# A 16-head attention of a decoder rewritten from a loop over sequences to one unrolled stream of 64 head pairs

## The reference, cut to what matters

```python
h = layernorm(x)                                  # no weights, eps 1e-5
q = (h @ Wq + bq) / 8;  k = ctx @ Wk + bk;  v = ctx @ Wv + bv     # 128 -> 1024 features, 16 heads of 64
p = softmax(q @ k.T + mask)                       # per sequence and head, 256 x 256
x = x + concat_heads(p @ v) @ Wo + bo             # 1024 -> 128
```

## Time and profile before

| | us |
|---|---|
| median of 3 runs (2844.6 to 2848.43) | 2846.11 |
| the profiled execution | 2847.98 |
| its span in the profile | 2846.2 |
| PE busy in the span | 1904.2 (67%) |
| PEld busy | 1116.7 (39%) |
| DVE busy | 1594.2 (56%) |
| ACT busy | 951.7 (33%) |
| POOL busy | 152.7 (5%) |

### The profile page before, as it was taken

The page is one execution under the profiler, slowest core; times in us unless marked ns, Lnnn a source line. Parts: engine busy times, 40 slices in busy tenths (PEclk is TensorE's granted clock), DMA queues, the critical chain, the costliest instruction groups (busy, mean ns, idle before and its releaser), DMA issues. The chain is left out here.

```text
span 2846.2 us, 37625 instructions
## 1 busy us (share of the span) xinstructions
PE 1904.2 (67%) x12470; PEld 1116.7 (39%) x12470; DVE 1594.2 (56%) x5577; ACT 951.7 (33%) x1872; POOL 152.7 (5%) x162
## 2 busy tenths in 40 slices
PE   3897689367864489923234777767798888558922
PEld 1554334234543345511123444444454444333410
DVE  5665368444444466667666666565623333457854
ACT  1553267231211145422002444444432222116721
POOL 2110021000000032000000000000000000002100
PEclk9998799678976689955557998898998989559965
DMA  3100120000000011000001000000000000002000
GB/s 89 22 13 1 45 35 12 8 1 0 0 6 0 26 23 24 2 11 0 38 0 79 4 4 4 4 7 4 5 1 0 0 0 6 0 14 28 13 0 15
DMA packets 22000, 38.52 MB, mean 14 GB/s; under 512 B 2176, under 2 KB 17536, under 8 KB 20864
## 3 DMA queue, kind: packets, MB, share of 16 engines
q1 hardware_dynamic: 20160, 35.47, 5.2%
q10 hardware_dynamic: 1728, 1.57, 0.4%
HBM read 23.40 MB, written 1.05 MB: 9 GB/s over the span
## 5 line engine op out<-in xcount | busy, mean ns | idle before, releaser
L434 DVE TENSOR_REDUCE L_xattn_nmax<-ps 128x4 f32<-128x1024 f32 x192 | 234.6, 1222 | 126.3 <-PE ps L663 124.8
L543 ACT ACTIVATE L_xattn_probs<-ps 128x1024 f32<-128x1024 f32 x192 | 196.6, 1024 | 126.7 <-PE ps L696 125.2
L2122 ACT ACTIVATE wide_pr<-wide_sc,wide_nm 128x256 f32<-128x256 f32 x256 | 127.9, 500 | 133.0 <-DVE wide_nm L2074 113.5
L1179 DVE SCALAR_TENSOR_TENSOR moe_z_sb<-ps,weights,moe_a_sb 128x512 f32<-128x512 f32 x64 | 47.7, 750 | 173.8 <-ACT moe_a_sb L1197 173.7
L2070 DVE CUSTOM_DVE_ANT_0 wide_sc<-ps,wide_mask 128x256 f32<-128x256 f32 x256 | 97.3, 417 | 67.3 <-PE ps L2162 67.3
L1231 PE MATMUL ps<-moe_z_sb,weights 128*128 128x512 f32 x256 | 123.5, 628 | 8.9 <-DVE moe_z_sb L1179 8.9
L2173 PE MATMUL ps<-const,wide_pr 128*128 128x128 f32 x512 | 90.1, 302 | 36.9 <-DVE wide_pr L2080 36.9
L810 PE MATMUL ps<-L_xattn_parts,lay 128*128 128x512 bf16 x288 | 96.9, 406 | 18.3 <-ACT L_xattn_parts L620 17.2
L712 PE MATMUL ps<-L_xattn_probs,values 128*32 128x256 f32 x1536 | 102.8, 385 | 1.6 <-ACT L_xattn_probs L543 1.6
L2162 PE MATMUL ps<-wide_k,wide_q 64*128 64x256 f32 x512 | 71.9, 405 | 45.4 <-DVE wide_nm L2074 37.9
L309 POOL TENSOR_TENSOR L_xattn_rest<-L_xattn_full,L_xattn_parts 128x512 f32<-128x512 f32 x24 | 27.7, 1156 | 1312.9 <-ACT L_xattn_parts L620 1312.9
(11 more groups left out here) (485 smaller groups left out, 4322.6 us busy)
## 6 DMA issues: line engine op xcount, KB each, us to landing
keys<-L_xattn_parts SPq DMA_DIRECT2D x126, 64.0 KB
weights<-in_packed_L_ffn SPq DMA_DIRECT2D x2, 2608.0 KB, 12.2
keys<-L_attn_parts SPq DMA_DIRECT2D x42, 64.0 KB
weights<-in_packed_L_xattn SPq DMA_DIRECT2D x2, 1316.0 KB, 7.1
wide_mask<-in_mask SPq DMA_DIRECT2D x8, 256.0 KB, 2.7
const<-in_packed_const SPq DMA_DIRECT2D x1, 1677.5 KB, 9.7
weights<-in_packed_L_ffn SPq DMA_DIRECT2D x1, 1540.5 KB, 10.4
weights<-in_packed_L_ffn SPq DMA_DIRECT2D x1, 1540.0 KB, 6.6
```

The lines of the kernel that those rows point to most:

```text
L434: v.tensor_reduce(nm, ps[:, BANK_M:BANK_M + 2, :].rearrange("p j (t n) -> p j t n", t=2), AX.X, ALU.max, negate=True).then_inc(S("m_used"), 1)
L543: a.activation(probs[:, s % RING, :, :, :].rearrange("p j t n -> p j (t n)"), ps[:, BANK_P:BANK_P + 2, :], ACT.Exp, scale=HD ** -0.5)\
L2122: ins = a.activation(pr[:, h % 2, qt, :], sc[:, h % 2, qt, :], ACT.Exp, bias=nm[:, h % 2, qt:qt + 1], accum_out=sums[:, h % 2, qt:qt + 1])
```

## The change

The loop and its blocks go. The sublayer is one block, unrolled over 64 slots (8 sequences of 8 head pairs), and every engine walks through the places tau = -16 to 79. In place s PE turns the probabilities of slot s-2 (8 transposes), makes the scores of slot s+1 in one pair of banks, and weighs slot s-2; DVE masks slot s (4 operations), copies the first head of the turned slot s-2, negates the maxima of slot s (one operation for the pair), and normalises slot s-1 (4 operations); ACT copies the weighed slot s-3, the second head of the turned slot s-2, and takes the exponentials of slot s (4 operations). So half of the copies of turned probabilities move from DVE to ACT.

Beside this, in the same places: q and k of slot s+2 are projected into one bank (one pair of matmuls per place) and copied by ACT in the next place; V of the next sequence is projected in positions 1 to 4 through one bank, and copied by DVE in positions 2 to 5; that bank also takes the transposed LayerNorm output of the next sequence (position 5) and the product with Wo of the sequence before (positions 6 and 7), which DVE adds to x at position 0 of the window after. The statistics of the LayerNorm of sequence n+2 are interleaved with DVE's operations in positions 4 and 5, the normalised rows are made by ACT in position 6 instead of by DVE, and the bias bo is added to x by POOL. The context is read in place rather than copied. The scaling of bq and the load of the next weights move into the same block, and the masks have two buffers and are loaded ahead, behind the next weights in SP's queue. The lines that the change adds, with "..." where some are left out (declarations of buffers, Newton's iteration, which is as before, and the removed lines, which are printed above):

```diff
+    SLOTS = SEQS * M
+    BANK_S, BANK_T, BANK_V, BANK_A, BANK_B = 0, 2, 4, 6, 7
+    QK = 6
+    half = [slice(DK * j, DK * j + DK) for j in range(2)]
...
+        places = [Place(tau, M, SEQS) for tau in range(-2 * M, SLOTS + 2 * M)]
+        def projected(tau):
+            n, t = divmod(tau, M)
+            m = n + (t >= QK)
+            return (m if 0 <= m < SEQS else None), (t - QK) % M
+        with C.turn() as block:
...
+                at = ks.index(k)
+                if at + 1 < len(ks):
+                    load_weights(C, sp, ks[at + 1], packed)
+                for m in range(SEQS):
+                    if m >= 2:
+                        sp.wait_ge(S("scores_used"), 4 * M * (m - 1))
+                    sp.dma_start(mask[:, m % 2, :, :], maskd[:, m * 2 * SEQ:(m + 1) * 2 * SEQ]
+                                 .rearrange("p (t n) -> p t n", t=2)).then_inc(S(("even_mask", "odd_mask")[m % 2]), 16)
...
+                g.wait_ge(C.weights_loaded[k], 32)
+                g.tensor_scalar(bq[:, :], w("bq"), DK ** -0.5, None, ALU.mult).then_inc(S("bias_scaled"), 1)
+                for m in range(SEQS):
+                    g.wait_ge(S("xn_ready"), 2 * (m + 1))
+                    x3 = xp(m).rearrange("p (t d) -> p t d", d=D)
+                    g.tensor_tensor(x3, x3, bcast(w("bo"), 1, [P, 2, D]), ALU.add).then_inc(S("bo_added"), 1)
...
+                def prepare(m):
+                    for t in range(2):
+                        yield L.tick(v.bn_stats(stats[:, t, :], C.x[:, m * SEQ + t * D:m * SEQ + (t + 1) * D]))
+                    L.settle()
+                    one = mv[:, m % 2, :, :]
+                    for t in range(2):
+                        yield L.tick(v.bn_aggr(one[:, t, :], stats[:, t, :]))
+                    L.settle()
+                    first, shift = rstd[:, m % 2, 0, :], rstd[:, m % 2, 1, :]
+                    yield from newton(first, one[:, :, 1], 2)
+                    yield v.scalar_tensor_tensor(shift, one[:, :, 0], -1.0, first, ALU.mult, ALU.mult)\
+                        .then_inc(S("rstd_ready"), 1)
+                def masked(s, j):
                     for qt in range(2):
+                        v.tensor_tensor_reduce(out=sc[:, s % 2, j, qt, :], in0=ps[:, BANK_S + j, qt * SEQ:(qt + 1) * SEQ],
+                                               in1=mask[:, s // M % 2, qt, :], scale=1.0, scalar=-3.0e38, op0=ALU.add,
+                                               op1=ALU.max, accum_out=mx[:, s % 2, 2 * j + qt:2 * j + qt + 1])\
+                         .then_inc(S("scores_used"), 1)
+                v.wait_ge(C.weights_loaded[k], 32)
+                side = iter(())
+                for p in places:
+                    s = p.tau
+                    m = p.job(4, 2)
+                    if m is not None:
+                        side = prepare(m)
+                    live = 0 <= s < SLOTS
+                    if live:
+                        v.wait_ge(S("scores_ready"), s + 1)
+                        if s % M == 0:
+                            v.wait_ge(S(("even_mask", "odd_mask")[s // M % 2]), 16 * (s // M // 2 + 1))
+                        masked(s, 0)
+                        next(side, None)
+                        masked(s, 1)
+                    next(side, None)
+                    if 0 <= s - 2 < SLOTS:
+                        v.wait_ge(S("prT_ps"), s - 1)
+                        v.tensor_copy(prT[:, s % 2, 0, :, :].rearrange("p t n -> p (t n)"), ps[:, BANK_T, :])\
+                         .then_inc(S("prT_first"), 1)
+                    next(side, None)
+                    if live:
+                        v.wait_ge(S("scores_used"), 4 * (s + 1))
+                        v.tensor_scalar(nm[:, s % 2, :], mx[:, s % 2, :], -1.0, None, ALU.mult).then_inc(S("masked"), 1)
+                    if 0 <= s - 1 < SLOTS:
+                        r = s - 1
+                        v.wait_ge(S("exp_done"), r + 1)
+                        inverted = L.tick(v.reciprocal(inv[:, r % 2, :], sums[:, r % 2, :]))
+                        next(side, None)
+                        L.upto(inverted)
+                        for j in range(2):
+                            for qt in range(2):
+                                one = pr[:, r % 3, j, qt, :]
+                                v.tensor_scalar(one, one, inv[:, r % 2, 2 * j + qt:2 * j + qt + 1], None, ALU.mult)\
+                                 .then_inc(S("normalised"), 1)
+                                next(side, None)
+                    for n in range(4):
+                        m = p.job(n + 2, 1)
+                        if m is not None:
+                            v.wait_ge(S("v_proj"), 4 * m + n + 1)
+                            if m >= 2 and n == 0:
+                                v.wait_ge(S("pv_ready"), M * (m - 1))
+                            cols = slice((n % 2) * 512, (n % 2) * 512 + 512)
+                            v.tensor_tensor(V[:, m % 2, n // 2, cols], ps[:, BANK_B, :], w("bv")[:, cols], ALU.add)\
+                             .then_inc(S("v_ready"), 1)
+                    m = p.job(0, -2)
+                    if m is not None:
+                        v.wait_ge(S("out_ready"), m + 1)
+                        v.wait_ge(S("bo_added"), m + 1)
+                        v.tensor_tensor(xp(m), xp(m), ps[:, BANK_B, 0:SEQ], ALU.add).then_inc(S("added"), 1)
+                    if p.t == 5:
+                        for _ in side:
+                            pass
...
+                a.wait_ge(C.weights_loaded[k], 32)
+                a.wait_ge(S("bias_scaled"), 1)
+                for p in places:
+                    s = p.tau
+                    if 0 <= s - 3 < SLOTS:
+                        r = s - 3
+                        a.wait_ge(S("pv_ready"), r + 1)
+                        if r >= 2 * M and r % M == 0:
+                            a.wait_ge(S("out_ready"), r // M - 1)
+                        a.activation(attT[:, r // M % 2, r % M, :], ps[:, BANK_V + r % 2, 0:SEQ], ACT.Copy)\
+                         .then_inc(S("attT_ready"), 1)
+                    m = p.job(6, 1)
+                    if m is not None:
+                        a.wait_ge(S("hT_ps"), m + 1)
+                        a.activation(hT[:, :], ps[:, BANK_B, 0:SEQ], ACT.Copy).then_inc(S("hT_ready"), 1)
+                    m, u = projected(p.tau - 1)
+                    if m is not None:
+                        a.wait_ge(S("qk_proj"), M * m + u + 1)
+                        a.activation(q[:, u % 4, :], ps[:, BANK_A, 0:SEQ], ACT.Identity, bias=bq[:, u:u + 1],
+                                     scale=DK ** -0.5)
+                        a.activation(kk[:, u % 4, :], ps[:, BANK_A, SEQ:2 * SEQ], ACT.Identity,
+                                     bias=w("bk")[:, u:u + 1]).then_inc(S("qk_copied"), 1)
+                    if 0 <= s - 2 < SLOTS:
+                        a.wait_ge(S("prT_ps"), s - 1)
+                        a.activation(prT[:, s % 2, 1, :, :].rearrange("p t n -> p (t n)"), ps[:, BANK_T + 1, :], ACT.Copy)\
+                         .then_inc(S("prT_second"), 1)
+                    if 0 <= s < SLOTS:
+                        a.wait_ge(S("masked"), s + 1)
+                        for j in range(2):
+                            for qt in range(2):
+                                n = 2 * j + qt
+                                ins = a.activation(pr[:, s % 3, j, qt, :], sc[:, s % 2, j, qt, :], ACT.Exp,
+                                                   bias=nm[:, s % 2, n:n + 1], accum_out=sums[:, s % 2, n:n + 1])
+                        ins.then_inc(S("exp_done"), 1)
+                    m = p.job(6, 2)
+                    if m is not None:
+                        a.wait_ge(S("rstd_ready"), m + 1)
+                        if m:
+                            a.wait_ge(S("hT_ps"), m)
+                        for t in range(2):
+                            a.activation(xn[:, t, :], C.x[:, m * SEQ + t * D:m * SEQ + (t + 1) * D], ACT.Identity,
+                                         bias=rstd[:, m % 2, 1, t:t + 1], scale=rstd[:, m % 2, 0, t:t + 1])\
+                             .then_inc(S("xn_ready"), 1)
...
+                pe.wait_ge(C.weights_loaded[k], 32)
+                def scores(s):
+                    u = s % M
+                    pe.wait_ge(S("qk_copied"), s + 1)
+                    if s:
+                        pe.wait_ge(S("scores_used"), 4 * s)
                     for qt in range(2):
                         for j in range(2):
+                            mm = pe.matmul(ps[:, BANK_S + j, qt * SEQ:(qt + 1) * SEQ],
+                                           q[half[j], u % 4, qt * P:(qt + 1) * P], kk[half[j], u % 4, :],
                                            start=True, stop=True)
+                    mm.then_inc(S("scores_ready"), 1)
+                def turn(s):
+                    if s:
+                        pe.wait_ge(S("prT_first"), s)
```

(73 more changed lines are left out.)

183 lines of the change are left out of this document (34 added, 149 removed).

## The result

The changed kernel takes 2696.65 us (median of 4 runs, 2695.32 to 2697.72), the kernel before 2847.27 beside it (4 runs, 2844.6 to 2855.98): a ratio of 0.9466, 95% interval 0.9445 to 0.9487. Forecast were 2671 us and a range of 2636 to 2710. The kernel is faster and its time lies inside the range, but 25.6 us above the forecast: the saving is some 150 us where 175 were predicted.

A forecast was written before the change was run, and what follows sets the result against it. PE was taken to become the bound of the merged stream. Head 23, places 308.3 and tail 10.3 give a stage of 341.6 us against 516.9, saving 175.3: 2671 us against the median, range 2636 to 2710.

The forecast's parts named there:

- head: Stretch from the stage's first DVE operation to PE's first turning, paid once: 22.8 us, taken as 23.
- places 2 to 63: Eight windows of 40.7 us, 326 us, less work missing in the first and last and places 0 and 1: 308.3 us.
- tail: End of the stage, last copy to weighing and attT, then product with Wo and add, paid once: 10.3 us.
- PE is the bound: In the new stream PE replaces DVE as the bound: 40.2 of a window's 40.7 us, DVE working 30.8.
- The price of a place: PE's turn, q, scores, k and weighing take 4.1 us, with 0.1 to 0.2 lost at each of four group changes.
- packed rival: PE runs its groups without gaps and V's handover hides: a window of 37.0 us, 2642 us in all; chance 0.14.
- second ring: Chain from DVE's copy through exponentials, attT, q and k copies to PE's next q: no place under some 4.2 us.
- rival of rings: Waits through four engines set every place, PE idle about 0.6 us in each, 5.7 on average: 2708 us; chance 0.26.
- Positions: The eight places of one sequence's window, priced singly by their side work: from 4.2 to 5.93 us, sum 40.7.
- POOL: Adds of bo on POOL are off every chain: 0 us in the sum, 4.4 us as the bound if they delay DVE.
- clock rival: PE idles often and briefly and is granted half speed: 9.5 us a place, 2960 us in all; chance 0.02.
- The overlap: Neighbouring slots run at once on the engines, a window taking 40.7 us; without it 7.85 us a place, 2847; chance 0.02.

The follow-up runs named there:

- e4: DVE normalises only 64 of each 256 columns of the probabilities, against the changed kernel: stage 357.9 us against 358.4.
- e5: PE projects q and k of only 128 of the 256 tokens, against the changed kernel: stage 338.9 us against 358.4.
- e6: DVE copies both turned matrices of a pair and ACT none, against the changed kernel: stage 372.6 us against 358.4.
- e2: PE projects q and k after the weighing instead of around the scores, against the changed kernel: 2680.7 us, stage 343.7 against 358.4.
- e1: ACT copies q and k before attT instead of after it, against the changed kernel: 2685.53 us, stage 348.3 against 358.4.
- e7: e3 with the first sequence's four V parts in four idle banks instead of one: 2675.96 us, stage 338.6 against 342.2.
- e3: Both order edits, e1 and e2, together on the changed kernel: 2679.15 us, stage 342.2 against 358.4.
- e8: e7 with LayerNorm's operations moved to other positions and the last sequence's product with Wo started early: 2677.53 us, stage 337.4 against 338.6.

## Why the prediction held, and where it missed

**The miss in terms.** From the profiled executions 2672.7 was the forecast and 2696.15 came, +23.5. The stage is +16.8 (358.4 against 341.6): head +7.1 (30.1 against 23), places 2 to 63 +9.5 (1558.18 to 1875.98 is 317.8, against 308.3), tail +0.3. The unchanged code behind has +8.5, in front -2.0.

**PE is the bound (right).** The signs were given for the stage: PE over 90% busy at clock 0.98 or more, DVE 75 to 80%. It is 96% at 0.96, and DVE 70%; the stream alone has 98% at 1.00, and DVE 74%. What misses is the head at half clock, not the bound. e4 shows it from DVE's side, e5 from PE's, and e5 and e6 show that DVE is close behind where V is added.

**The price of a place, 4.1 with gaps at changes of group (right).** Plain places without the ring are 4.17 (turn 0.93, q 0.53, scores 1.06, k 0.63, weigh 1.02) against 0.9, 0.55, 1.07, 0.55, 1.0. e2 shows that the gaps at changes are real, 0.15 to 0.2 each, and single pairs in its trace show that the scores' 0.2 over 0.86 lies at the two changes beside them, as the prediction read it. The packed rival is out.

**The second ring, 4.2 (the step that failed).** The prediction followed it from DVE's copy through the exponentials to attT, q and k, and said that these copies end before PE asks except in position 1. The sum of durations was fair; what it left out is that attT's copy first waits for this place's weighing, the last thing PE does, and the copies of q and k stand behind it. The ring that closes is 4.62. It shows wherever neither a V part nor Wo lies between weighing and the next turning: position 1 +0.6, position 6 +0.7, plain places +0.4. Window by window that is 42.0 us against 40.7. e1 removes it by an exchange of program order alone: 10.1 us, more than the 9.5 by which the places missed. The rival of rings had thus a part of the truth, in 20 of 62 places and not in all.

**Positions.** 0: 4.11 (4.2 forecast); 2 to 4: 5.07 (4.96, 4.96, 5.2); 5: 4.45 (4.6); 7: 6.00 (5.93); 1: 5.58 (4.96); 6: 6.65 (5.93). That LayerNorm makes position 4 wait for V's add was wrong for the changed kernel (no wait in its 5.07) and appears at 5.06 once the rest is faster (e2, e5).

**The head, 23 (mis-sized by 7.1).** LayerNorm and the V rounds end 12.4 us in, forecast 11.7; a round takes 2.86 for 2.65. From there to the next q projection 4.2 (3.65 forecast), to the end of the first scores 3.2 (2.3). The last part is the step that failed: 5.2 forecast, 10.4 measured (1547.80 to 1558.18). The prediction followed DVE through two maskings and the normalising. It left out that PE makes a k and a q projection between the two scores, at 1.2 GHz (scores 2.08) and with a wait for the copies of q and k (0.93), and that PE's whole work of place 1, 5.1 us, stands in front of the first turning. An exponential's table load of 1.28 us lies there too; ACT waits for PE behind the exponentials that follow it (0.92), so it is covered. Four banks for V (e7) brought only 3.6, since the mask was late next.

**The clock.** It stayed at 1.00 in the whole stream, with PE idle for 6.3 of 321.8 us in 21 waits, all but one of 0.2 to 0.4. The Trainium skill, "TensorE: Matmul & The Clock Gate", section "A second HAM failure mode: psum-queue depth-cycling", ties such moments between groups to a swinging clock; this stream, which changes banks with every group, does not show it.

**POOL.** The adds of bo take 0.72 us each, 5.8 in all, where the prediction halved a larger add and had 4.4 as its bound. The Trainium skill, "SBUF — State Buffer", section "Who interferes with whom", speaks of a lock between DVE and GpSimd; whether it costs anything here no row shows, because DVE is busy for 0.00 us in each of the eight stretches in which an add runs. The term is 0 in the changed kernel for this reason.

**Readings and sums.** The second ring's 5.2 less 0.9 is 4.3 and not 4.2. Of the waits of 1.11 and 0.83 us named for the rival of rings, 1.11 is ACT's and only 0.83 PE's. The clock rival's 9.5 us a place gives 2671 + 62 x 4.4 = 2944 and not 2960. None of the three changes the forecast.

**The overlap (right).** A sequence takes 42.0 us, against 64.8 a turn before.

**What is best.** e3, two changes of order, takes the stage from 358.4 to the forecast's 342. e7 and e8 have the shortest stages, 338.6 and 337.4; as programs e3, e7 and e8 (0.9412, 0.9395 and 0.9402 of the kernel before) can't be told apart by their intervals.

## What to carry to other kernels

When several loops are merged into one software-pipelined place, follow each ring in program order on every engine: a copy that waits for the latest result of the place must stand last on its engine, or all that stands behind it inherits its wait. Group work of one tile shape together on PE; each change of shape cost 0.15 to 0.2 us here. Price the fill of a new pipeline at the clock that the trace shows for such stretches and along each engine's program order, and ask of each transfer that was hidden by the old head whether the new one still hides it.

## What the runs showed of the hardware

The gap on PE between groups follows the change of tile shape and not the semaphore waits: k, V and turning follow each other without a gap, V and turning behind waits, while each change between the whole array and its halves costs 0.2 us, 0.1 on either side of it, and the change into the 128x64 groups 0.15 (e2). The clock granted in identical, unchanged code differs from execution to execution, 0.89 or 0.91 to 0.92 in the same stretch, and 5 to 6 us of 800 go with it, in the kernel before as in the changed one. The mask's DMA, usually landed after 2.6 us, takes 15.4 when it is issued behind the next stage's weights (e7).
